# Attention's steps in another order, in a vision tower on one core

## What is computed

```python
h = _L0_tok_ref(x, ...)     # three Haar levels, each detail band weighed by a softmax over the image, rebuilt
h = _layernorm(h + _L0_attn_ref(h, ...))
h = _layernorm(h + _L0_ffn_ref(h, ...))
...
Q, K, V = (proj(Wq, bq), proj(Wk, bk), proj(Wv, bv))       # per image: 256 tokens, 16 heads
attn = jax.nn.softmax(jnp.einsum('bhqd,bhkd->bhqk', Q, K) * scale, axis=-1)
out = jnp.einsum('bhqk,bhkd->bhqd', attn, V)               # then @ Wo.T + bo
```

## Time and profile before

| | us |
|---|---|
| median of 3 runs | 1596.23 |
| lowest and highest | 1588.97, 1597.39 |
| the profiled execution: its time | 1596.87 |
| the profiled execution: its span | 1595.1 |

### The profile page before, as it was taken

The page is one execution under the profiler, slowest core; times in us unless marked ns, Lnnn a source line. Parts: engine busy times, 40 slices in busy tenths (PEclk is TensorE's granted clock), DMA queues, the critical chain, the costliest instruction groups (busy, mean ns, idle before and its releaser), DMA issues.

```text
span 1595.1 us, 23616 instructions
## 1 busy us (share of the span) xinstructions
PE 1306.6 (82%) x6856; PEld 916.3 (57%) x6856; DVE 927.7 (58%) x2735; ACT 523.6 (33%) x998; POOL 697.3 (44%) x912
## 2 busy tenths in 40 slices
PE   1368978877989875999999818888888399999997
PEld 0245555554656543666667516666666266666665
DVE  6555775676676635555555546778776344444443
ACT  1024444434555431222222135555554121111111
POOL 6551444526222124545544324554454434444443
PEclk9578789789999756999999957787777699999999
DMA  6457345544575323121211052321100361110100
GB/s 161 86 100 95 61 88 115 81 76 88 119 144 118 86 81 128 61 66 61 64 62 63 22 171 80 105 93 57 57 14 21 129 232 31 30 32 29 29 19 12
DMA packets 88747, 126.33 MB, mean 79 GB/s; under 512 B 17696, under 2 KB 71598, under 8 KB 87600
## 3 DMA queue, kind: packets, MB, share of 16 engines
q1 hardware_dynamic: 68832, 85.13, 24.0%
q0 software_dynamic: 16416, 38.46, 7.8%
q10 hardware_dynamic: 3376, 1.22, 0.4%
HBM read 71.24 MB, written 31.54 MB: 64 GB/s over the span
## 4 chain that ended last, share of the span: by engine, by line
PE 58%; DVE 16%; POOL 11%; issue 6%; DMA 4%; ACT 3%; SPq 2%; ACTq 0%; DVEq 0%; POOLq 0%
PE ebank L1931 9%; PE ebank L1942 8%; PE ebank L1158 8%; PE ebank L1170 8%; PE bank L591 3%; DVE top_a_a L961 2%; PE av_bank L647 2%; PE mbank L1492 2%; PE ebank L1952 2%; PE ebank L1180 2%; PE bank L673 2%; POOL rows_d L1431 2%; PE s_bank L614 2%; POOL rstd_m_m L1407 2%; PE s_bank L635 2%
## 5 line engine op out<-in xcount | busy, mean ns | idle before, releaser
L961 DVE TENSOR_REDUCE top_a_a<-s_bank 128x4 f32<-128x1024 f32 x128 | 156.5, 1223 | 111.5 <-PE s_bank L614 108.1
L790 ACT ACTIVATE prob_a<-s_bank 128x1024 f32<-128x1024 f32 x128 | 130.4, 1019 | 77.2 <-PE s_bank L635 75.3
L1931 PE MATMUL ebank<-w,exT 128*128 x312 | 142.2, 599 | 0.7 <-ACT exT L1977 0.7
L1492 PE MATMUL mbank<-w2T_m,fhT_m 128*128 128x256 f32 x512 | 142.7, 442 | 0.0
L1942 PE MATMUL ebank<-w,ehT 128*128 x624 | 141.2, 379 | 0.9 <-ACT ehT L1985 0.9
L1158 PE MATMUL ebank<-w,exT 128*128 x284 | 135.5, 600 | 0.6 <-ACT exT L1205 0.6
L1170 PE MATMUL ebank<-w,ehT 128*128 x568 | 134.4, 380 | 0.8 <-ACT ehT L1211 0.8
L1492 PEld LDWEIGHTS mbank<-w2T_m,fhT_m 128*128 128x128 f32 x512 | 118.7, 232 | 23.1
L1117 POOL DMA_INDIRECT ex<-rows_d,tile_row x71 | 72.4, 1020 | 127.7 <-DVE ey L1244 109.3
L1942 PEld LDWEIGHTS ebank<-w,ehT 128*128 128x128 f32 x624 | 115.6, 190 | 15.7 <-issue 1.6
L525 POOL DMA_INDIRECT rows_d<-h_a,row_i_a x64 | 63.7, 995 | 135.1 <-DVE row_i_a L1046 120.1
(11 more groups left out here) (349 smaller groups left out, 2646.3 us busy)
## 6 DMA issues: line engine op xcount, KB each, us to landing
w<-in_L_ffn_W SPq DMA_DIRECT2D x16, 1024.0 KB, 10.7
qs_a<-parts_q_a SPq DMA_DIRECT2D x96, 128.0 KB, 4.5
ks_a<-parts_k_a SPq DMA_DIRECT2D x96, 128.0 KB, 6.4
w<-in_L_ffn_w SPq DMA_DIRECT2D x16, 512.0 KB, 5.7
image_a<-in_x SPq DMA_DIRECT2D x4, 1024.0 KB, 7.4
h_d<-rec_a SPq DMA_DIRECT2D x4, 1024.0 KB, 3.8
x_a<-h_d SPq DMA_DIRECT2D x16, 256.0 KB, 5.1
ya_m<-y_d SPq DMA_DIRECT2D x16, 256.0 KB, 2.8
```

The source lines that it names most:

```text
L790: nc.scalar.activation(prob[:, j % 4].rearrange("p g t s -> p (g t s)"), s2_bank[:].rearrange("p g s -> p (g s)"), ACT.Exp, scale=HD ** -0 ...
L961: nc.vector.tensor_reduce(top[:, j].rearrange("p g t -> p (g t)"), s1_bank[:].rearrange("p g (t s) -> p (g t) s", t=TPI), axis=AX, op=ALU. ...
L1492: last = nc.tensor.matmul(b[:, t * D:(t + 1) * D], hT[:, f, t * P:(t + 1) * P], w2T[:, f, :], start=False, stop=f == FC - 1)
L1931: last = nc.tensor.matmul(bank[1 + n % 2][:], xT[j % 2][:, ch, :], w[:, bass.ds(e, 1), at:at + 512].rearrange("p a f -> p (a f)"), start=c ...
```

## The change

The code of every step stays; only the list `STEPS` is replaced. The eight slots of the pairs remain. What lies otherwise, on all engines at once:

- `av_3` (and `tsum`, `tsm`) go ahead of `p2_0`; `rk` goes behind `q`; `ot_1` into the first slot; `p1_1`, `p1_2`, `p1_3` each go a slot forward, and slot 3 has no `p1`.
- `shift_1` is done at the head of the next turn (`t`, behind `p1_0`) instead of at the end of its own (`n`, behind `p1_7`); `sw_1` stays in that next turn.
- `v` goes from slot 4 to slot 5, `xT` from slot 7 to slot 4, `xb` from the head of the turn to its end.
- `ld` goes behind `sw_1`, `stq` and `stk` a slot later, `tokin` behind both stacks and `sw_0`.
- `otv_0` and `lg` go to the last slot; `tprd_0` to `tprd_6` are done before `p1_7`, `tgate` and `tok` a slot later.

```diff
-        STEPS = [("ld", "n2"), ("tokin", "n2"), ("weights", "o"),
-                 ("p2_0", "t"), ("av_3", "p"), ("p1_0", "n"), ("xb", "n2"), ("rk", "o"), ("tsum", "n2"), ("q", "f"), ("rows", "o"), ("sw_1", "t"), ("qlo", "f"),
-                 ("tsm", "n2"),
-                 ("p2_1", "t"), ("p1_1", "n"), ("ot_1", "p"), ("otv_1", "p"), ("k", "f"), ("stq", "f"),
-                 ("p2_2", "t"), ("texp", "n2"), ("klo", "f"), ("av_0", "t"), ("p1_2", "n"), ("tgate", "n2"), ("tprd_0", "n2"), ("aT", "p"), ("stk", "f"),
-                 ("p2_3", "t"), ("out", "p"), ("p1_3", "n"), ("shift_0", "n"), ("res", "p"), ("tprd_1", "n2"), ("tok", "n2"),
-                 ("p2_4", "t"), ("av_1", "t"), ("sw_0", "n"), ("v", "f"), ("p1_4", "n"), ("nrm", "p"), ("tprd_2", "n2"),
-                 ("p2_5", "t"), ("ot_0", "t"), ("p1_5", "n"), ("otv_0", "t"), ("tprd_3", "n2"), ("hT", "p"),
-                 ("p2_6", "t"), ("av_2", "t"), ("p1_6", "n"), ("tprd_4", "n2"), ("lg", "p"),
-                 ("p2_7", "t"), ("xT", "n2"), ("p1_7", "n"), ("shift_1", "n"), ("route", "p"), ("tprd_5", "n2"), ("tprd_6", "n2")]
+        STEPS = [("weights", "o"), ("av_3", "p"), ("tsum", "n2"), ("tsm", "n2"),
+                 ("p2_0", "t"), ("p1_0", "n"), ("q", "f"), ("shift_1", "t"), ("rk", "o"), ("ot_1", "p"), ("rows", "o"), ("p1_1", "n"), ("sw_1", "t"),
+                 ("otv_1", "p"), ("qlo", "f"),
+                 ("p2_1", "t"), ("k", "f"), ("p1_2", "n"),
+                 ("p2_2", "t"), ("ld", "n2"), ("klo", "f"), ("aT", "p"), ("stq", "f"), ("p1_3", "n"),
+                 ("p2_3", "t"), ("stk", "f"), ("texp", "n2"), ("out", "p"), ("tprd_0", "n2"), ("shift_0", "n"), ("av_0", "t"), ("res", "p"),
+                 ("tgate", "n2"),
+                 ("p2_4", "t"), ("sw_0", "n"), ("tprd_1", "n2"), ("tprd_2", "n2"), ("p1_4", "n"), ("av_1", "t"), ("nrm", "p"), ("tprd_3", "n2"),
+                 ("xT", "n2"), ("tokin", "n2"), ("tok", "n2"),
+                 ("p2_5", "t"), ("ot_0", "t"), ("tprd_4", "n2"), ("p1_5", "n"), ("v", "f"), ("tprd_5", "n2"), ("hT", "p"),
+                 ("p2_6", "t"), ("p1_6", "n"), ("av_2", "t"),
+                 ("p2_7", "t"), ("tprd_6", "n2"), ("otv_0", "t"), ("p1_7", "n"), ("lg", "p"), ("route", "p"), ("xb", "n2")]
```

## The result

| | before | after |
|---|---|---|
| median, us | 1592.6 (4 runs) | 1518.76 (4 runs) |
| lowest and highest | 1588.32, 1597.39 | 1516.92, 1521.42 |
| profiled execution: span, us | 1595.1 | 1519.3 |
| mean granted clock over the span | 0.863 | 0.894 |

The ratio is 0.954, with a 95% interval of 0.950 to 0.958: 74 us faster, outside the range of 1530 to 1590. The sign and most of the named waits came as forecast; the gain is 1.7 times the sum of 43 us.

What follows compares the result with a forecast made beforehand. PE was taken to bound a quiet attention turn, busy 22.83 of 25.77 us. Terms of -28, -4, -4, -5 and -2 summed to -43 us, giving 1553 us, with 8 in 10 for 1530 to 1590.

Steps and rivals of the forecast that it cites:

- quiet turn, thirteen times: Thirteen attention turns: PE's stalls mostly go, a quiet turn falls from 25.77 to 23.6 us, together -28 us.
- named waits of the wavelet turns: Turns with wavelet work: `tsum` -10, shifts' rows -13, `hT` -4.7, products +15, POOL's lateness +9; sum -4 us.
- the clock in these turns: Thirteen turns: of some 32 us put down to TensorE's low clock, 4 come off and 28 stay.
- start: Before the thirteen turns: POOL analyses the next images earlier, so `tsum` waits less; 5.2 us at most, taken as -5.
- turns 16 and 17, and the end of attention: Turn 16 has the quiet turn's gain, -2 us; turn 17 counts nothing, the last image's path 0.
- two lags of 7 us remain: Clock in the thirteen turns: two lags of 7 us still stand, so just 4 us come off.
- The bounds of the terms: Turn 11 us better or 28 worse, clock 14 better or 4 worse, lags 8 either way; all best called unlikely.
- The first: Head of the turn, DVE's queue: the gain turns into new waits; 1575 to 1592 us, chance 0.18.
- The second: Slower: PE granted 1.2 GHz through much of every turn; 1618 us at clock 0.76, chance 0.08.
- break-even of 0.82: Mean clock at which a new turn, with 0.8 us of waits and 1.8 of lags, equals the earlier 30.5 us.
- The third: No change, 1589 to 1604 us: products and POOL hold up 12 and 9 us, head loses half its gain; chance 0.08.
- The block of up to 1.3 us: Turns 5 and 9: by the shared port `xb` would block one DVE product up to 1.3 us, together 2.6.

Runs made afterwards that it cites:

- runs with useless matmuls: Useless matmuls put into PE's waits, no step moved: in the kernel before 1582.87 us, 0.990 of before; in the new order 1512.87 us, 0.946 of before.
- the root's move: New order, but in turns 7 and 11 POOL takes the root ahead of the late `xb` and the four sends of rows: 1503.94 us, 0.941 of before.
- the kernel with the images' steps alone: New list, but `tokin`, `tsum`, `tsm`, `texp`, `tgate`, `tok` and the products about where the kernel before has them: 1535.57 us, 0.962 of before.
- the wavelet steps alone: Old list, but `tokin`, `tsum`, `tsm`, `texp`, `tgate`, `tok`, `xb` and the products in their new places: 1581.86 us, 0.991 of before.

## Why the forecast was too small

**Named waits: nearly right.** `rk`, the first shift and `p1_5` lost their waits; `p1_3` got one of 0.49 (0.4 said) and `k` waits about 0.1 (0.25 said). `tsum` lost its 9.9 us (rows 7) but for 0.86 once; turns 5 and 9 became DVE-bound, with DVE 30.08 us busy in turn 5, and they take 8.2 and 6.7 us more than a quiet one (7.4 each said; their clocks of 0.89 and 0.94 are in it). The shifts' rows no longer hold up turns 7 and 11; `hT` waits 3.48 us twice (4.5 said) for the root behind the sends. `nrm` beside POOL's analysis takes 3.48 us in turn 8, and `hT`, behind `v`, no longer waits for it. Not foreseen were waits of 0.6 us for the low part of Q ahead of `aT` in turns 5, 7, 9 and 11, and of 0.8 for the first shift in 7 and 11. x is never late, and `tsum` is at 76.0 us. Turn 3 begins 5.8 us sooner (5 said).

**What failed is the size of three terms**, all missed to the same side: the end of attention (put at 2 us, measured 16), the quiet turn and the clock. By the two profiled executions:

| term | said | measured |
|---|---|---|
| quiet turn, thirteen times | -28 | -36.4 |
| named waits of the wavelet turns | -4 | -6.7 |
| the clock in these turns | -4 | -10.8 |
| start | -5 | -5.8 |
| turns 16 and 17, and the end of attention | -2 | -15.9 |
| sum | -43 | -75.6 |

- *The quiet turn* fell by 2.80 us instead of 2.15. I had taken PE's busy time of 22.83 us as a floor and put 0.8 of new waits on it. Busy time was no floor: it fell to 22.4 (67.07/3) for the same matmuls. I read this from how the profile counts: an instruction that overlaps its neighbour when PE is dense counts in full beside a wait, so a wait that goes takes some tenths of busy time with it. The new waits are 0.6, not 0.8.
- *The named waits and the clock.* The thirteen turns held 342.2 - 13 x 22.97 = 43.6 us beyond quiet turns, where they had held 61.1. Summed over PE's timelines, waits of over 0.1 us beyond the quiet turn's 2.9 and 0.6 went from 28.3 to 21.6. The rest, put down to the clock because nothing else is left, went from 33 to 22. The forecast took 4 off and kept 28. The step that failed is "two lags of 7 us remain, and the product turns get PE still less busy": it looked at the turns with a lag only. The turns between them gained: turn 4 stands at 1.00 instead of 0.76, turn 8 at 0.92 instead of 0.85, turn 12 at 0.93 instead of 0.89, with 0.6 us of idle time in each where they had 3.7, 5.5 and 1.7. And the product turns 5 and 9, with 4.8 us of idle time instead of 3.5, did not fall either: they stand at 0.89 and 0.94 instead of 0.85 and 0.87. The runs with useless matmuls, and the root's move, show that PE's waits lower the clock here; that they alone decide it is not shown.
- *Turns 16 and 17 and the end* are the largest miss, 14 us, and here the step that failed is the zero: I had counted nothing for turn 17 ("PE has too little work") and nothing for the end, on the ground that its path keeps its steps, and had not looked at what the low clock there costs. Turn 17 went from 27.83 to 21.90 us with its clock from 0.69 to 0.84, turn 16 from 27.6 at 0.88 to 22.5 at 1.00, and from `p2_0` of turn 18 to the last `rk` 42.2 us at 0.58 became 37.3 at 0.71. In the kernel with the images' steps alone the same stretch, 459.3 to the last `rk` at 539.4, takes 80.1 us (81.7 after); with the wavelet steps alone 97.5 (97.6 before). So it is the images' order. The whole stretch, before and after:

```profile
501.90:599.50 97.60, 79.58 (x547) 49.87 (x548) 50.42 (x183) 38.26 (x61) 19.54 (x24) 0.70 0.32 83
```
```profile
442.20:523.90 81.70, 66.92 (x534) 44.00 (x530) 48.19 (x176) 37.91 (x60) 19.55 (x24) 0.83 0.38 100
```

  PE's idle time fell from 18.0 to 14.8 us only. The other 12.7 us are busy time, 1.1 of it the `av_3` that changed sides, the rest nearly the same matmuls in less time at a clock of 0.83 instead of 0.70. So most of this gain came through the clock. Why the clock stayed up longer there stays open.
- *The range.* The bounds of the terms, 11, 14 and 8 us better, add up to 1520, about where the measured 1518.76 lies. I had called that unlikely and drawn the line at 1530, as if the terms erred by themselves. But fewer waits also meant a higher clock, so two of them moved together, and the bounds had no room at all for the end of attention.

**The rivals.** The first (new waits at the head of the turn) did not come: turn 6, at a clock of 0.87, has the same 0.6 us of idle time as a quiet turn. The second pointed at the right thing with the wrong sign: the clock moved, upward. Its break-even of 0.82 was never near. The third needed product turns 12 us and `hT` 9 us late each; they were 6.7 to 8.2 and 3.5.

**The shared port.** DVE's timeline of turn 8 after, `nrm` beside POOL's analysis, takes 3.48 us (0.73 in a quiet turn). This trace agrees again with the rule of the Trainium skill, SBUF — State Buffer, Who interferes with whom, that VectorE and GpSimd hold their shared port pair exclusively:

```profile
251.76 3.48 DVE L1008 TENSOR_SCALAR h_a<-res_a,moments_a_a,rstd_a_a 128x256 f32<-128x256 f32 x2
```

The block of up to 1.3 us that I had put on a product in turns 5 and 9 did not come. The large products there take 1.19 to 1.27 us (1.18 in rows 5). By the times it was POOL that was held up: in turn 5 the two instructions of the root, beside two products, take 1.13 and 1.71 us (0.24 and 0.73 in turn 4), and `nrm`, beside `xb`, takes 1.14 instead of 0.73. POOL, then DVE:

```profile
162.19 1.13 POOL L520 TENSOR_SCALAR rstd_a_a<-moments_a_a 128x2 f32<-128x2 f32 x1 [3.61 <-DVE moments_a_a L999]
163.41 1.71 POOL L521 TENSOR_TENSOR rstd_a_a<-rstd_a_a,minus_half 128x2 f32<-128x2 f32 x1
165.09 1.27 POOL L516 TENSOR_TENSOR xb_a<-x_a,bo_a 128x512 f32<-128x512 f32 x1
```
```profile
163.27 1.24 DVE L848 CUSTOM_DVE_ANT_0 product_a<-fine_a,weight_a 128x768 f32<-128x768 f32 x1
...
165.69 1.14 DVE L1008 TENSOR_SCALAR h_a<-res_a,moments_a_a,rstd_a_a 128x256 f32<-128x256 f32 x2
```
